# Second attention of a small vision transformer: who forms the low halves of the expert weights, and when

## The reference

```python
def attn(hidden):                       # 12 heads of width 8, causal
    q, k, v = split(hidden @ W_attn + b_attn, 3)
    q, k, v = q @ P_q, k @ P_k, v @ P_v             # 192 -> 96
    w = softmax(mask(q_h @ k_h.T / sqrt(8)))
    return (w @ v_h) @ W_back @ W_proj + b_proj

def ffn(x):                             # 8 experts, top 2, and a shared one
    gates = top2_softmax(x @ Wr.T)
    moe = sum_e gates[e] * (relu(x @ W1[e].T + b1[e]) @ W2[e].T + b2[e])
    return moe + 0.2 * (relu(x @ sW1.T + sb1) @ sW2.T + sb2)

h = h + attn(layernorm(h))
h = h + ffn(layernorm(h))
```

## Time and profile before

| | us |
|---|---|
| median of three runs | 936.61 (934.75 to 936.91) |
| the profiled execution, device time | 938.55 |
| its span from first to last instruction | 936.8 |
| projection, about | 555 to 607 |
| row maxima, about | 607 to 644 |
| mixing, about | 644 to 697 |

### The profile page before, as it was taken

How to read it: one execution, slowest core, us unless ns; L and a number is a source line. 1 busy time by engine, 2 the same in 40 slices (tenths; PEclk the granted TensorE clock), 3 DMA queues, 4 the chain that set the end, 5 groups by cost and what they waited for, 6 DMA issues and landing times. The chain is left out here.

```text
span 936.8 us, 19693 instructions
## 1 busy us (share of the span) xinstructions
PE 681.2 (73%) x7374; PEld 518.8 (55%) x7375; DVE 655.2 (70%) x1370; ACT 639.4 (68%) x1217; POOL 309.8 (33%) x250
## 2 busy tenths in 40 slices
PE   2675472244199655989999938756965898999995
PEld 1553240122077423469999934434544467999994
DVE  3488999999779898865454548777669785554542
ACT  1468955999799686877455526897844752977672
POOL 6730750000000000047887544400001202777854
PEclk9798555555589786899999967955986899999998
DMA  6444772000033223943333355602645932233422
GB/s 200 145 90 120 233 245 69 0 17 9 1 103 103 94 85 115 338 123 68 65 61 56 34 149 225 222 22 72 252 157 186 335 149 76 58 63 61 63 34 30
DMA packets 61478, 106.06 MB, mean 113 GB/s; under 512 B 9725, under 2 KB 43144, under 8 KB 61144
## 3 DMA queue, kind: packets, MB, share of 16 engines
q1 hardware_dynamic: 45016, 88.48, 28.6%
q0 software_dynamic: 16384, 16.53, 11.3%
HBM read 77.20 MB, written 27.77 MB: 112 GB/s over the span
## 5 line engine op out<-in xcount | busy, mean ns | idle before, releaser
L2412 DVE SCALAR_TENSOR_TENSOR m_hT<-m_pu,m_unit,m_hT 128x512 f16<-128x512 f32 (+1 forms) x138 | 86.3, 663 | 21.3 <-ACT m_hT L2368 21.3
L1140 ACT ACTIVATE a_ex<-m_pieces,a_nb 128x256 bf16<-128x256 f16 x192 | 94.3, 497 | 5.4 <-DVE a_nb L1166 5.4
L2404 DVE COPY m_xgT<-m_px 128x768 f16<-128x768 f16 (+1 forms) x46 | 22.8, 496 | 102.5 <-PE m_px L2250 102.5
L2375 ACT ACTIVATE m_pu<-m_pu,m_b,m_unit 128x256 f32<-128x256 f32 (+1 forms) x138 | 63.7, 507 | 44.6 <-PE m_pu L2282 42.7
L979 PE MATMUL a_pp<-a_room 16*128 16x256 bf16 x240 | 55.9, 412 | 40.5 <-DVE m_pieces L1154 31.9
L2368 ACT ACTIVATE m_hT<-m_pu,m_unit 128x512 f16<-128x512 f32 (+1 forms) x138 | 81.3, 634 | 0.0
L2213 POOL DMA_INDIRECT m_xg<-xn_d,m_token x70 | 68.9, 985 | 35.2 <-issue 18.9
L2379 ACT ACTIVATE m_pu<-m_pu,m_unit 128x512 f32<-128x512 f32 (+1 forms) x69 | 41.1, 596 | 52.1 <-PE m_pu L2282 52.1
L2225 POOL DMA_INDIRECT out_h<-m_yo,m_token x39 | 62.1, 1592 | 31.3 <-DVE m_yo L2422 18.1
L2225 POOL DMA_INDIRECT h_d<-m_yo,m_token x39 | 62.1, 1591 | 25.5 <-DVE m_yo L2422 10.0
L2282 PE MATMUL m_pu<-m_xgT,m_pieces 128*128 128x256 f16 (+1 forms) x690 | 69.5, 260 | 0.9 <-DVE m_xgT L2404 0.9
(11 more groups left out here) (494 smaller groups left out, 1678.0 us busy)
## 6 DMA issues: line engine op xcount, KB each, us to landing
m_pieces<-in_m_w SPq DMA_DIRECT2D x11, 768.0 KB, 5.1
a_early_w<-in_m_w SPq DMA_DIRECT2D x10, 768.0 KB, 5.4
hv_raw<-in_m_w SPq DMA_DIRECT2D x8, 768.0 KB, 7.1
w1h_d<-hv_parts SPq DMA_DIRECT2D x8, 768.0 KB, 4.0
m_w<-w1h_d SPq DMA_DIRECT2D x8, 768.0 KB, 9.1
m_pieces<-in_m_w SPq DMA_DIRECT2D x8, 576.0 KB, 5.5
a_room<-in_m_w SPq DMA_DIRECT2D x8, 576.0 KB
hv_raw<-in_m_w SPq DMA_DIRECT2D x8, 576.0 KB, 6.7
```

The costliest lines, as they stand in the source:

```text
L1140: last = act.activation(ex[:, n % 2, r], v16t[:, n, r, :], ACT.Exp, bias=nbt[:, n, r:r + 1], scale=scale, accum_out=sumst[:, n, r:r + 1])
L2375: act.activation(pu[:, u, n, q * w:(q + 1) * w], pu[:, u, n, q * w:(q + 1) * w], ACT.Relu, bias=b1[:, bass.ds(e * FC + 2 * n + q, 1)], sca ...
L2412: last = v.scalar_tensor_tensor(hT[:, u, 1, third], pu[:, u, n, 0:2 * w], unit[:, 1:2], hT[:, u, 0, third], ALU.mult, ALU.subtract)
```

## The change

In the projection ScalarE no longer scales the raw piece and GpSimd no longer forms low halves. VectorE forms them from the raw piece, the scale and the high half in one instruction, the one it has always used in the mixing: pieces 0 and 1 around `low(1)`, 2 and 3 around `low(2)`, 4 in front of the two `weigh`, 5 behind `low(3)` and before `take(3)`. `Halves.MIXED` goes from 8 to 9: in the mixing pieces 6, 7 and 8 are split in front of the images, pieces 9 to 15 behind images 0 to 6, and nothing is split behind image 7. SP's order follows the same constant, so that the store of piece 8 and the fetch of piece 12 now stand before the second half of the rows. One semaphore is no longer there.

```diff
-    COUNT, FRONT, MIXED, RAW, PARTS = 2 * E, 6, 8, 4, 3
+    COUNT, FRONT, MIXED, RAW, PARTS = 2 * E, 6, 9, 4, 3
...
-    def scale(self, act, n):
-        raw, parts, scale = self.tiles(n)
-        act.wait_ge(self.highs, n + 1)
-        act.activation(raw, raw, ACT.Identity, scale=scale).then_inc(self.scaled, 1)
-
-    def low(self, pool, n):
-        raw, parts, scale = self.tiles(n)
-        pool.wait_ge(self.scaled, n + 1)
-        self.c.nc.gpsimd.tensor_tensor(parts[:, 1, :], raw, parts[:, 0, :], ALU.subtract).then_inc(self.lowered, 1)
...
+    def split_low(self, dve, n):
+        raw, parts, scale = self.tiles(n)
         dve.wait_ge(self.highs, n + 1)
         self.c.nc.vector.scalar_tensor_tensor(parts[:, 1, :], raw, scale, parts[:, 0, :], ALU.mult, ALU.subtract)\
             .then_inc(self.lowered, 1)
...
-                        for n in range(Halves.FRONT):
-                            halves.low(pool, n)
...
                                 halves.high(act, n)
-                                halves.scale(act, n)
...
                         norm(2)
+                        halves.split_low(dve, 0)
                         low(1)
+                        halves.split_low(dve, 1)
...
                         norm(3)
+                        halves.split_low(dve, 2)
                         low(2)
+                        halves.split_low(dve, 3)
...
                         take(2)
+                        halves.split_low(dve, 4)
                         for n in range(2):
                             weigher.weigh(dve, n)
                         low(3)
+                        halves.split_low(dve, 5)
                         take(3)
```

More of the change, by code:

```diff
@@ L2619, in __init__ @@
         self.put = [c.sem(f"hv_put{i}") for i in range(self.PARTS)]
-        self.highs, self.scaled, self.lowered = (c.sem(f"hv_{n}") for n in ("highs", "scaled", "lowered"))
+        self.highs, self.lowered = (c.sem(f"hv_{n}") for n in ("highs", "lowered"))
     def tiles(self, n):
@@ L2640, in high, with split_high @@
         act.activation(parts[:, 0, :], raw, ACT.Identity, scale=scale).then_inc(self.highs, 1)
-    def scale(self, act, n):
-        raw, parts, scale = self.tiles(n)
-        act.wait_ge(self.highs, n + 1)
-        act.activation(raw, raw, ACT.Identity, scale=scale).then_inc(self.scaled, 1)
-    def low(self, pool, n):
-        raw, parts, scale = self.tiles(n)
-        pool.wait_ge(self.scaled, n + 1)
-        self.c.nc.gpsimd.tensor_tensor(parts[:, 1, :], raw, parts[:, 0, :], ALU.subtract).then_inc(self.lowered, 1)
-    def split(self, dve, n):
+    def split_high(self, dve, n):
         raw, parts, scale = self.tiles(n)
@@ L2660, in split @@
             .then_inc(self.lowered, 1)
+    def split(self, dve, n):
+        self.split_high(dve, n)
+        self.split_low(dve, n)
     def store(self, sp, n):
```

## The result

The changed kernel takes 929.33 us (median of four runs, 929.16 to 931.63) against 935.68 for the kernel before in the same comparison (four runs): a ratio of 0.9931, with a 95% interval of 0.991 to 0.9952. That is 6.3 us faster. The forecast was 934.9, with a range of 931.0 to 939.6, so the time lies 1.7 us under the range.

The account below looks back on a forecast made before the run. It took the projection to be bound by a ring of waits through ScalarE, and TensorE and ScalarE to go in step in the mixing. Projection -2.3, image 4 +3.4, tail -2.8 made -1.7 us: 934.9, range 931.0 to 939.6.

Parts of the forecast that it names:

- ScalarE's scaling stands on the ring: Projection: scaling instructions delay each 512-token group's cycle of engine waits; removing them gives 3.1 us by `project(2)`.
- The clock, one term of 1.4 us: Projection: TensorE's idle 1.54 us goes, its clock no longer falls, and `project(2)` takes 2.76 instead of 4.19 us.
- the case in which it also gains in `project(1)`: Rival, chance 0.12: clock holds through the projection, block gains 4.9 us, total 932.3.
- VectorE's low halves are late by 0.25 and 0.85: Projection: low halves 1 and 3 only partly fit VectorE's idle time, delaying the path 0.25 and 0.85 us.
- Low half 4 falls into idle time, low half 5 costs 1.1: Projection's last group: low half 4 is free before `low(3)`; low half 5 before `take(3)` costs 1.1 us.
- Block: -2.3 forecast: Projection as a whole: 3.4 us earlier less 1.1 gives 2.3 us; bounds 0.9 and 4.9.
- The copy of the row maxima: 1.0: Mixing's front: splitting piece 8 before VectorE's copy makes the sums of unit 4 start 1.0 us late.
- the rival: Clock falls while TensorE waits for the rows at image 4: 2.3 us more, total 937.2 or 939.4; chance 0.25.
- Image 4's rows: +3.4: Mixing: rows queue behind two more SP transfers (5.2 us), so image 4's scores start 3.4 us later; bounds 2.2 and 5.6.
- My slower bound: SP's queue in the mixing: at the slower mean rate, 2.75 MB in 11.3 us, the added 1.57 MB costs 6.5 us.
- The tail: -2.8: Mixing's end: a narrower piece behind image 6 saves 0.55 us and none behind image 7 saves 2.25.
- rows not late: Rival, chance 0.2: image 4's rows land in time, only the copy's 1.0 us remains, total -4.1 us, 932.5.

Follow-up runs that it names:

- e3: Kernel before without ScalarE's second (scaling) instruction of each split, GpSimd still forming low halves from the raw piece: 927.82 us, ratio 0.9913.
- e5: Changed kernel with ScalarE's second instruction of each split put back: 934.25 us against 936.37 for the kernel before, ratio 0.9987.
- e1: Changed kernel's projection with the old mixing: 930.7 us against 936.12 for the kernel before, ratio 0.996.
- e8: Changed kernel with piece 8 split behind the row maxima's copy, its store and fetch behind the rows in SP's queue: 928.92 us, ratio 0.993.
- a0: The changed kernel run once more, unaltered, for comparison on one chip: ratio 0.9934 to the kernel before.
- e9: Changed kernel with the rows put to DRAM ahead of piece 8's store and piece 12's fetch: 929.92 us, ratio 0.9937.
- e10: e8 with low halves 4 and 5 also moved to the start of the row maxima: 925.91 us against 936.01 for the kernel before, ratio 0.9899.
- e4: Kernel before with GpSimd's low halves left out, ScalarE keeping both instructions: 935.96 us, ratio 1.0002.
- e2: Kernel before (old projection) with the changed kernel's mixing: 936.6 us, ratio 0.9985.
- e7: Kernel before with only the last piece's store moved from the mixing into the block behind it: 933.89 us against 936.37, ratio 0.9971.
- e12: Kernel before with unused matmuls in TensorE's gaps in projection groups 0 to 2 only: 933.03 us against 936.7, ratio 0.995.
- e6: Kernel before with unused matmuls in TensorE's gaps in all four projection groups: 936.46 us against 936.37, ratio 0.9998.

## Why the prediction was wrong

It was wrong in size and not in direction. The two blocks were forecast at -1.7 us and measured -7.9 (-5.6 and -2.3). Of the 6.2 between them, 3.3 are the projection, where the clock was given 1.4, and 1.8 are image 4, which was given +3.4 for rows that it did not wait for; the tail has 0.5, and the last 0.5 lies between image 4 and the tail.

*ScalarE's scaling stands on the ring, 3.1 us by `project(2)`.* Right; e3 and e5 show it. In sum it is 4 to 5 us for three groups, by e5.

*The clock, one term of 1.4 us.* This is the first step that failed. The forecast let it hold only from `project(2)` on and gave the case in which it also gains in `project(1)` a chance of 0.12. In the changed kernel `project(1)` took 3.83 us against 5.33, and in the other traces without the scaling (e1, e3, e8, a0, e9, e10) 2.76 to 4.44, with `project(2)` at 2.76 to 4.1. That rival's own sign, `project(1)` under 4 us, was met in five of the seven traces. The two projections together took 6.55 to 7.20 us in all seven, 9.52 in the kernel before and 9.59 to 10.43 in e4, e2 and e7: so the term is 2.3 to 3.0 us against before's trace, 2.9 in the changed kernel, where the forecast had 1.4. x_low of group 3 came 33.75 us after the first statistics (589.95 - 556.20) and not 39.91 (594.90 - 554.99 in the earlier trace rows): 6.2 us earlier where the forecast had 3.4. Of the missing 2.8, 1.5 are `project(1)`, 0.7 a rise inside `project(0)` that belongs to this execution and not to the change (e2, with the old projection, has it too), and the rest low halves that were less late. e12 has the size of the term by itself: 3 us, from 38 to 39 down to 35.1. In the old ring, what the clock was worth was split over the groups, and the forecast read it off one of them.

*VectorE's low halves are late by 0.25 and 0.85.* About right, too high: 0.5 in sum is what is left of the 6.2 after the terms above and the scaling. It is a remainder; no run measures it.

*Low half 4 falls into idle time, low half 5 costs 1.1, so what ScalarE saves in the last group is lost.* Right in kind. From x_low of group 3 to the block's end 0.5 of the gain were lost. Against a last group without the two (8.2 in e3, e10 and e12) they cost 2.5 to 3.4 us. The 0.9 between these is the clock once more: behind the same wait of 2.12 us for `low(3)`, the twelve matmuls of `spread_heads(3)` ran at full clock in the changed kernel and in e1, and took 4.4 us in a0, e8 and e9, as here in e8:

```profile
595.84 4.44 PE L2909 MATMUL a_pq<-a_once,a_room 96*128 96x512 f16 x12 [2.12 <-DVE a_once L3022]
```

*Block: -2.3 forecast, -5.6 measured.* The bound that I had given for it was 4.9, so in this pair of traces the block lay outside. With a0 (48.9) it is -4.1; by the means of three traces with the old projection (before, e2, e7: 54.0) and five with the new (48.3) it is -5.7.

*The copy of the row maxima: 1.0.* Right against this trace, and too low for the wait. The sums of unit 4 began 10.4 us after the block's first scores in the kernel before and 11.4 in all five traces with piece 8 before the copy: 1.0 late. But TensorE's wait was 2.32, 2.24, 1.91, 1.79 and 1.70 us. The forecast took TensorE's time of arrival from a trace in which its clock was low until unit 3; when it rises earlier, TensorE is at unit 4 sooner (9.2 us in e7 and e10) and the fixed work of VectorE in front of it costs more. And the clock fell after this wait in the changed kernel and in e2 (the second set of sums behind it took 1.50 us in both; 0.85 in a0, e5 and e9), where the rival had looked for it at image 4.

*Image 4's rows: +3.4.* This is the second step that failed. The wait in the queue was right and its size was not. The rows did wait for what was issued before them: 5.9 us in e9 against 9.0 in a0. The Trainium skill ("DMA: Bandwidth & Descriptors", section "Queues, rings and completion order") has a DMA engine consume in ring order what SP issued, and these two runs agree with it. But two more transfers delayed the reads by 2.6 us (17.4 to 20.0 after the block's first scores), by 3.6 between e9 and a0, and not by 5.2: from 651 to 657 us the DMA moved 402 to 432 GB/s, where I had put 332. (My slower bound also has a slip: from 649.68 to 661.34 are 11.7 us and not 11.3.) After the reads' start image 4 could begin 4.0 us later in a0, so the last read lands within 2.0 us, where I took 2.3. SP's wait, forecast at some 11 us, was 7.7, and in the changed kernel image 4 did not wait for the rows at all. Its scores stand at 23.4 us before (667.38 - 643.96) and 25.0 after (664.52 - 639.54): 1.6 late. Of this 1.0 is the copy at unit 4 and some 1.5 the fall of the clock behind it; 0.9 is taken off because the kernel before lost that much itself between images 0 and 1, most of it in a stop without a releaser:

```profile
658.98 0.29 PE L3097 MATMUL a_pb<-identb,a_mask 32*128 32x64 bf16 x11 [0.72 <-issue]
```

*The tail: -2.8, "with no unknown in it".* There was one: SP's issue of the last store, 0.9 us by e7. From the turning of image 7 (693.22 in the earlier trace rows) to the output projection were 4.7 us before and are 2.0 now (689.26 to 691.27), and TensorE's wait for the copy fell from 3.20 to 2.60: 3.3 us. Of this, 0.7 lies between VectorE's last instruction and TensorE's first (1.3 before, 0.6 now), which the forecast had at nothing.

*The range.* Its low end took one good case at a time (projection high, or rows not late). Both came true together, the first in large part; by the forecast's own terms that is -4.9 + 1.0 - 2.8 = -6.7, or 929.9, and a range from single cases doesn't reach a sum of two.

## What to carry to other kernels

Where TensorE's work sits in a ring of waits, look for the instruction that other engines do inside the ring for someone else's sake, and take that out first; the engine with the conspicuous slow instructions may be hidden. A ring that gets shorter gains a second time if TensorE's clock stops falling in its gap, so give that term its own row, for every group and not only for the one whose matmuls show a change. And put side work into the idle time of a block that another engine bounds (here 4.2 us at its start) and not in front of a copy that TensorE waits for.

## What the runs showed of the hardware

Matmuls that nobody uses, put into TensorE's gaps, made the kernel before 3.7 us faster with the same results (e12): the granted clock stayed at 2.4 GHz and twelve matmuls took 2.76 us where they took 4.19 to 5.33. The same matmuls at a place where nothing follows cost what they take (e6, 2.1 us more in the last group).

The granted clock can fall after a single wait between stretches of busy work, and the wait's length alone does not tell whether it will. Behind the waits of 2.32 us (changed kernel) and 2.24 us (e2) at unit 4 the first sums ran in 0.85 us and the next in 1.50; behind the same wait at 1.91, 1.79 and 1.70 us (e5, a0, e9) all sums stayed at 0.85. Behind the wait of 2.12 us in the projection's last group the granted clock was 1.00 in the changed kernel and in e1, and 0.60 to 0.61 over the next 4.3 us in a0, e8 and e9, at the same place in the code and with the same work.
